# Weight parts of K/V tile 0 re-sorted over GpSimd and VectorE, batch 3's x measured in batch 2, and tile 1's products ahead of both h rows

## The reference, cut to what matters

```
mod = (silu(c) @ wmod).reshape(B, 6, 1, D);  sa, ca, ga, sb, cb, gb = mod[:, 0..5]
h  = layernorm(x) * (1 + ca) + sa
Xn = layernorm(h) * gamma + beta;  Q, K, V = split(Xn @ W_in + b_in)
K, V = rotary(K), rotary(V)
A  = 0.5 * sum_over_rows(K/|K| * V/|V|) + 0.5          # one vector of 512 per batch
x  = x + ga * ((A * Q) @ W_out + b_out + h)
h  = layernorm(x) * (1 + cb) + sb
x  = x + gb * (relu(h @ W_up.T) @ W_down.T + sum(softmax(top2(h @ W_gate.T))) * (h @ W_expert))
```

## Time and profile before

| | |
|---|---|
| median of 3 runs | 363.78 us (363.32 to 365.0) |
| profiled execution, its own time | 365.14 us |
| its span, first to last instruction | 363.4 us |
| TensorE busy (matmul) | 353.1 us, 97% |
| TensorE weight loads | 288.5 us, 79% |
| VectorE / ScalarE / GpSimd | 247.9 / 159.1 / 126.6 us |
| granted TensorE clock | 1.000 over the whole span |

### The profile page before, as it was taken

The page is one execution under the profiler, slowest core; times in us unless marked ns, Lnnn a source line. Parts: engine busy times, 40 slices in busy tenths (PEclk is TensorE's granted clock), DMA queues, the critical chain, the costliest instruction groups (busy, mean ns, idle before and its releaser), DMA issues.

```text
span 363.4 us, 4952 instructions
## 1 busy us (share of the span) xinstructions
PE 353.1 (97%) x1794; PEld 288.5 (79%) x1794; DVE 247.9 (68%) x508; ACT 159.1 (44%) x301; POOL 126.6 (35%) x131
## 2 busy tenths in 40 slices
PE   8799999999999999999999999999999999999996
PEld 5257587788777788888888898988988898889885
DVE  2689999979977778786977469338623852382474
ACT  1296838647169501476018753444234423441110
POOL 0395879777726166243531324800100010000000
PEclk9999999999999999999999999999999999999999
DMA  6998482370120000000000003101100110011003
GB/s 182 388 406 317 194 318 89 137 213 0 25 63 2 0 2 29 1 1 2 0 31 0 0 2 115 32 0 58 60 0 2 58 59 2 0 60 58 2 1 115
DMA packets 10985, 27.45 MB, mean 76 GB/s; under 512 B 1216, under 2 KB 1600, under 8 KB 9808
## 3 DMA queue, kind: packets, MB, share of 16 engines
q1 hardware_dynamic: 10960, 27.13, 21.1%
HBM read 22.90 MB, written 4.23 MB: 75 GB/s over the span
## 4 chain that ended last, share of the span: by engine, by line
PE 60%; DVE 12%; ACT 8%; issue 7%; DMA 5%; POOL 5%; SPq 2%; POOLq 0%; DVEq 0%; ACTq 0%
PE ps L1225 19%; PE ps L1227 19%; PE ps L1226 19%; PE ps L1284 2%; DMA gate_bc<-mod_rows 2%; DMA xs<-in_X 2%; POOL w_lo L414 2%; DVE hb L815 1%; DVE hst L825 1%; ACT z L626 1%; POOL hrs L411 1%; ACT ps L638 1%; DMA mod_rows<-xs 1%; ACT ps L585 1%; ACT z L617 1%
## 5 line engine op out<-in xcount | busy, mean ns | idle before, releaser
L1225 PE MATMUL ps<-wv_hi,t_hi 128*128 128x260 f32 (+1 forms) x192 | 61.7, 322 | 0.9 <-POOL wv_lo L414 0.5
L1227 PE MATMUL ps<-wv_hi,t_lo 128*128 128x260 f32 (+1 forms) x192 | 61.4, 320 | 0.0
L1226 PE MATMUL ps<-wv_lo,t_hi 128*128 128x260 f32 (+1 forms) x192 | 61.4, 320 | 0.0
L1225 PE MATMUL ps<-w_hi,g_hi 128*128 128x512 f32 (+1 forms) x132 | 51.2, 388 | 0.0
L1225 PE MATMUL ps<-t_hi,w_hi 128*128 128x512 f32 x128 | 50.6, 396 | 0.1
L1227 PE MATMUL ps<-w_hi,g_lo 128*128 128x512 f32 (+1 forms) x132 | 50.6, 383 | 0.0
L1226 PE MATMUL ps<-w_lo,g_hi 128*128 128x512 f32 (+1 forms) x132 | 50.6, 383 | 0.0
L1227 PE MATMUL ps<-t_hi,w_lo 128*128 128x512 f32 x128 | 50.0, 390 | 0.0
L1226 PE MATMUL ps<-t_lo,w_hi 128*128 128x512 f32 x128 | 49.9, 390 | 0.0
L1225 PEld LDWEIGHTS ps<-wv_hi,t_hi 128*128 128x128 f32 x192 | 36.1, 188 | 5.1 <-POOL wv_lo L414 1.4
L411 POOL TENSOR_TENSOR hrs<-hve,expo 128x4 f32<-128x4 f32 (+2 forms) x12 | 11.1, 923 | 81.9 <-DVE hve L832 62.8
(11 more groups left out here) (153 smaller groups left out, 703.8 us busy)
## 6 DMA issues: line engine op xcount, KB each, us to landing
stage<-in_w SPq DMA_DIRECT2D x5, 1024.0 KB, 4.8
out<-xs SPq DMA_DIRECT2D x15, 256.0 KB, 2.0
xs<-in_X SPq DMA_DIRECT2D x3, 1024.0 KB, 9.5
xs<-in_wmod SPq DMA_DIRECT2D x8, 256.0 KB, 5.9
stage<-in_w SPq DMA_DIRECT2D x8, 256.0 KB, 8.1
xs<-in_wmod SPq DMA_DIRECT2D x2, 1024.0 KB, 7.7
gate_bc<-mod_rows SPq DMA_DIRECT2D x8, 256.0 KB, 3.9
gate_bc<-in_wmod SPq DMA_DIRECT2D x1, 1024.0 KB, 13.3
```

The lines of the kernel that those rows point to most:

```text
L1225: mm(dst, l_hi, r_hi, start=start, stop=False)
L1226: mm(dst, l_hi, r_lo, start=False, stop=False)
L1227: return mm(dst, l_lo, r_hi, start=False, stop=stop)
```

## The change

Three edits come together.

1. In K/V tile 0 of batch 0 ScalarE rounds V's chunk 0 ahead of the first normalisation, K's chunk 1 ahead of the first evacuation and V's chunk 1 right behind it. GpSimd takes the lower part of K's chunk 1 ahead of `rstd_x0(2)`. The lower part of V's chunk 3 goes from GpSimd to VectorE, behind row tile 3's `h_row0`.
2. x of batch 3 is measured by VectorE in batch 2, as x of batch 2 is in batch 1: four statistics between the lower query parts, aggregation, shift after tile 0's products; ScalarE normalises it after tile 0's sums of squares of batch 2. ScalarE's two passes and the small steps are gone, and `rstd_x(3)` stands on GpSimd at the end of batch 1, behind `base`.
3. In batches 1 and 2 `h_row(b + 1, 0)` stands behind `kv_products(b, 1)`, with the other three, and no longer between `kv_sum(b, 0)` and `kv_rows(b, 1)`.

```
 GpSimd, attention(b)
                     weight(b, 1)
-                    if b + 2 < B:
-                        rstd_x(b + 2)
                     rstd_h(b + 1, 0, NT)
...
                         base(b + 1, t)
+                    if b == 1:
+                        rstd_x(3)
 GpSimd, start
             shift_h0(1)
+            low_kv(0, 1)
             rstd_x0(2)
-            low_kv(0, 1)
             low_kv(1, 1)
             low_kv(1, 2)
             low_kv(0, 3)
-            low_kv(1, 3)
             shift_h0(2)
 ScalarE, attention(b)
-                if b == 1:
-                    normalise_x(2)
-                    x_sums()
-                    x_squares()
+                if b < B - 1:
+                    normalise_x(b + 1)
                 norm_sums(b, 1)
...
-                if b + 2 < B:
-                    normalise_x(b + 2)
 ScalarE, start
             split_hi_kv(0, 0)
+            split_hi_kv(1, 0)
             normalise(0, 0, 1)
-            split_hi_kv(1, 0)
+            split_hi_kv(0, 1)
             t0_evac(0)
-            split_hi_kv(0, 1)
+            split_hi_kv(1, 1)
             normalise(0, 1, 1)
-            split_hi_kv(1, 1)
 VectorE, attention(b)
                     q_split(b - 1, c)
-                    if b == 1:
-                        x_row_stats(2, c)
-                if b == 1:
-                    x_aggr(2)
+                    if b < B - 1:
+                        x_row_stats(b + 1, c)
+                if b < B - 1:
+                    x_aggr(b + 1)
                 kv_rows(b, 0)
                 kv_products(b, 0)
-                if b == 1:
-                    x_shift(2)
+                if b < B - 1:
+                    x_shift(b + 1)
...
                 finish_rows(b - 1)
-                if b == 1:
-                    x_mean()
                 kv_sum(b, 0)
-                if b < B - 1:
-                    h_row(b + 1, 0)
-                else:
+                if b == B - 1:
...
                 kv_rows(b, 1)
-                if b == 1:
-                    x_var()
                 kv_products(b, 1)
                 if b < B - 1:
+                    h_row(b + 1, 0)
                     h_row(b + 1, 1)
...
                 kv_products(b, 2)
-                if b + 2 < B:
-                    x_shift(b + 2)
                 kv_sum(b, 2)
 VectorE, start
             h_row0(3)
+            split_lo_kv(1, 3)
             t0_split(1)
```

More of the change, by code:

```diff
@@ L102, in build @@
         nmu = xmn
-        xss = sb("xss", [P, NT])
         xst = sb("xst", [P, NT, 6])
@@ L116, in build @@
         sqj = sb("sqj", [P, D], mybir.dt.bfloat16)
-        xjunk = sb("xjunk", [P, D], mybir.dt.bfloat16)
         a_col = sb("a_col", [P, NC])
@@ L181, in build @@
         base_s = sem("base_s")
-        xsum_s = sem("xsum_s")
-        xmn_s = sem("xmn_s")
         kv_ps, kb_s, kv_sb = sem("kv_ps"), sem("kb_s"), sem("kv_sb")
@@ L589, in t0_evac @@
                                      ACT.Copy).then_inc(t_his, 1)
[L591 to L605, removed]
             def normalise_x1(t):
@@ L788, in x_aggr @@
                 v.tensor_scalar(xve[:], xmv[:, :, 1], EPS, None, ALU.add).then_inc(xve_s, 1)
[L790 to L797, removed]
             def x_shift(g):
@@ L801, in x_shift @@
                 wait(dve, xn_s, (g - 1) * NT)
-                if g < B - 1:
-                    v.scalar_tensor_tensor(xnm[:], xmv[:, :, 0], -1.0, xrs[:], ALU.mult, ALU.mult).then_inc(xnm_s, 1)
-                else:
-                    dve.wait_ge(xmn_s, 1)
-                    v.tensor_tensor(xnm[:], xmn[:], xrs[:], ALU.mult).then_inc(xnm_s, 1)
+                v.scalar_tensor_tensor(xnm[:], xmv[:, :, 0], -1.0, xrs[:], ALU.mult, ALU.mult).then_inc(xnm_s, 1)
             def h_row(g, t):
@@ L1078, in split_lo_kv @@
                 dve.wait_ge(wlo_v if i else wlo_k, k)
+                dve.wait_ge(wlo_v if i else wlo_k, k)
                 v.tensor_tensor(w_lo_of(W_ORDER[i], k), w_raw[i][:, k * D:(k + 1) * D],
```

## The result

| | before | changed kernel |
|---|---|---|
| median, 20 runs each, beside each other | 364.46 us (362.38 to 365.32) | 365.07 us (363.73 to 365.5) |
| ratio, 95% interval | | 1.0021 (1.0011 to 1.0031) |
| profiled execution: own time, span | 365.14, 363.4 | 363.73, 361.9 |
| VectorE / ScalarE / GpSimd busy | 247.9 / 159.1 / 126.6 | 249.3 / 153.5 / 124.7 |

The account below looks back on a forecast made before the run. TensorE (97% busy) bounds the kernel; only holes between its weight loads can be won. Arrival +0.2, batch 1 -1.0, batch 2 +0.35 sum to -0.4 us: profiled 365.14 to 364.7, median 363.78 to 363.4; range 361.3 to 365.3.

Parts of the forecast that it names:

- batch 1: -1.0 us forecast: Batch 1's total: -0.46 - 0.12 - 0.43 = -1.0 us, with ends -0.4 and -2.7.
- the moved work costs: Rival: VectorE loses the turn at 35.4, moved h row loses one at 90.5, batch 2 pays +0.6; +0.8, 364.6; chance 0.26.
- the turn at 35.4: Tile 0's product step against GpSimd's first scaling: VectorE first gives -0.2 us, GpSimd first loses 0.6.
- the wait for the gates: VectorE's wait for gates from DRAM; ending over 1 us away from 79.5 would show the forecast wrong.
- K/V tile 0: Batch 0's first tile: V 3 loads at 27.9 instead of 28.50; TensorE leaves about 0.5 us earlier, not 2.1.
- What arrives at batch 1: Delay or lead carried from tile 0 to batch 1's transposes: +0.2 us, with ends -0.5 and +1.1.
- -1.24: Batch 1, tile 3: the 1.28 us hole closes; about 0.8 of the 1.24 us is given back.
- -0.46: Batch 1, transposes at 105.93 for batch 2: 0.46 us earlier if VectorE's product step is first; hole grows to 1.6.
- +0.14: Batch 1, product step at 90.56: if GpSimd is first, the variance comes at 99.36, 0.14 us later; not taken.
- -0.12: Batch 1, 110.30: the x shift in front of tile 2's sum is gone, -0.12 us.
- -0.43: Batch 1's last lower query part comes 0.7 us earlier, closing the 0.47 us hole: -0.43 us.
- +0.35: Batch 2: h row behind tile 1's products costs at the second transposes, hole 0.21 becomes 0.5; ends 0 and +0.7.

Follow-up runs that it names:

- e11: e6 with rstd_x0(2) back in front of the lower part of K's chunk 1; 363.77 us, ratio 1.0000.
- e14: e13 with h_row(b+1, 0) back in front of tile 1; 362.81 us, ratio 0.9966.
- e5: Kernel before plus one tiny GpSimd product ahead of out_weight(1)'s subtraction, so VectorE is first at 57.7 us; 363.53 us, ratio 0.9986.
- e16: e14 without the K/V tile 0 part of the change; 363.44 us, ratio 0.9984.
- e4: Kernel before with only batch 3's x measured by VectorE in batch 2; 364.52 us, ratio 1.0001.
- e13: e6 with the 1 MB load of batch 3's x moved behind batch 3's modulation rows; 363.59 us, ratio 0.9986.
- e1: The changed kernel again, unaltered; 364.90 us, ratio 1.0018 to before.
- e6: Changed kernel plus the tiny GpSimd product of e5, so VectorE is first at 57.7 us; 363.97 us, ratio 1.0001.
- e8: Changed kernel plus the two tiny VectorE instructions of e7; 365.24 us, ratio 1.0026.
- e7: Kernel before plus two tiny VectorE instructions ahead of the weighted sum, so GpSimd is first at 57.7 us; 364.73 us, ratio 1.0019.
- e12: Kernel before with out_weight(1) behind weight(0, 3) on GpSimd, without a tiny instruction; 364.72 us, ratio 1.0019.

## Why the prediction was wrong

It forecast -0.4 us; it is +0.6 by the medians and +0.8 by the means. The step that failed is batch 1: -1.0 us forecast, +0.26 measured. Two terms were put at nothing, the toss at 57.7 us (about +0.3) and the end of the program (+0.29). The rival "the moved work costs" had the right sign. Of its three places the moved row in batches 1 and 2 was right; the turn at 35.4 was not lost: the changed kernel's product step there takes 0.29 us as before. It was won by a hair, with VectorE's step 0.01 us ahead of GpSimd's scaling, but in all ten traces with edit 1. One of the prediction's own signs of being wrong came true as well: the wait for the gates was to end within 1 us of 79.5, and the residual started at 77.28.

**K/V tile 0: right.** V's part 2 starts on GpSimd at 23.33, K's part 2 ends on VectorE at 25.18, V 3 loads at 27.37 with all times 0.45 us earlier than before from the start on (transposes at 17.51 against 17.96); forecast 23.8, 25.6, 27.9. Missed was that the first product comes 0.57 us later relative to those transposes, since a small VectorE step now lies behind GpSimd's split of K's part 1. The changed kernel, VectorE and GpSimd in tile 0 (timeline):

```profile
19.86 1.17 DVE L1011 TENSOR_SCALAR xve<-xmv 128x2 f32<-128x2 f32 x1
...
24.23 0.95 DVE L1035 TENSOR_TENSOR w_lo<-stage,w_hi 128x512 fp32r<-128x512 f32 x1
...
26.61 0.70 DVE L1035 TENSOR_TENSOR wv_lo<-stage,wv_hi 128x512 fp32r<-128x512 f32 x1
...
19.73 1.26 POOL L410 TENSOR_TENSOR w_lo<-stage,w_hi 128x512 fp32r<-128x512 f32 x1
...
23.33 1.31 POOL L410 TENSOR_TENSOR wv_lo<-stage,wv_hi 128x512 fp32r<-128x512 f32 x1 [0.26 <-ACT wv_hi L572]
...
26.59 0.55 POOL L407 TENSOR_TENSOR hrs<-hve,expo 128x1 f32<-128x1 f32 x1
```

**What arrives at batch 1: a term left out.** VectorE won the turn at 35.4, so the -0.2 of that order was there (transposes(1,0) 38.14 us after the first ones, 38.40 before). But I followed the edit only up to the transposes at 56.36 and took the end of batch 0 as it stood in one execution. There, at 57.7, lies a toss worth 1.2 us, which VectorE wins in about 44% of before's executions and in 16 to 22% of the changed kernel's. This term, about +0.3 on the mean, had no place in the sum, and the row that would have warned stood in the trace: two engines 0.05 us apart, one of them with a length of two turns. My ends for this part (+1.1) held its size, but for another meeting.

**Batch 1: the step that failed, wrong in sign, for two reasons.** The -1.24 at tile 3 and the -0.46 that was to be left of it rested on a hole that this execution had because its residual had waited 1.46 us for the gates. Of the 17 other traces 15 have no such wait, and without it there is no hole at tile 3 to close, with the h row in either place. VectorE then idles 2.67 us for TensorE with edits 2 and 3, where the forecast had 1 us, and +0.26 to +0.28 is lost. But the wait alone would not have saved it. e11 has a wait of 0.94 us and the moved row (timeline, VectorE, then weight loads):

```profile
79.15 1.29 DVE L881 TENSOR_TENSOR hb<-ps,hb 128x512 f32<-128x512 f32 x2 [0.94 <-DMA gate_bc<-mod_rows]
...
87.95 0.70 DVE L819 TENSOR_TENSOR ps<-ps,bkv_bc 128x512 f32<-128x512 f32 x1 [1.64 <-PE ps L1187]
...
90.77 0.83 DVE L836 TENSOR_TENSOR ps<-prod 128x128 f32<-128x128 f32 x1
91.98 3.02 DVE L780 TENSOR_TENSOR hb<-hb,sa_bc 128x512 f32<-128x512 f32 x2
```

```profile
105.68 0.86 PEld L1244 LDWEIGHTS ps<-idn,z 128*128 128x128 f32 x8 [1.59 <-ACT z L608]
```

Here the rows start 8.80 us after the residual, a microsecond sooner than elsewhere, and yet the transposes for batch 2 come 26.53 us after it, 0.11 later than with the h row in its old place. The product step is not first (0.83 us instead of 0.29) and the two rows lose another turn (3.02 instead of 1.27). The hole before the transposes is 1.59 us, close to the 1.6 that the forecast had for an execution with the wait. But the order is that of the branch which the prediction priced at +0.14 and did not take: I gave VectorE a tie on the strength of 0.04 us of replay.

**-0.12 and -0.43: not there.** From (2,0) to (2,2) it is 4.37 to 4.38 us with and without the x shift. The hole of 0.47 did close, but it was given back by batch 2's second transposes. With edit 2, VectorE's residual of batch 2 no longer waits for TensorE, its second gate step loses a turn (1.46 us against 0.79) and the first h row behind tile 1 waits for half a turn: 1.32 us in e14 at 138.42, where e5 has (timelines of e5, VectorE and weight loads):

```profile
127.45 0.69 DVE L919 TENSOR_TENSOR hb<-ps,hb 128x512 f32<-128x512 f32 x1 [0.57 <-PE ps L1230]
...
139.92 0.68 DVE L818 TENSOR_TENSOR hb<-hb,sa_bc 128x512 f32<-128x512 f32 x1
```

```profile
120.98 0.19 PEld L1228 LDWEIGHTS ps<-w_hi,g_hi 128*128 128x128 f32 x1 [0.45 <-DVE g_lo L910]
...
155.64 0.89 PEld L1287 LDWEIGHTS ps<-idn,z 128*128 128x128 f32 x8 [0.17 <-issue]
```

From (2,2) to (3,2) the kernel without edits 1 to 3 (e5) takes 47.05 us and e16, which has edit 2, 47.14: nothing is left of the 0.43. e4's ratio of 1.0001 says the same, within its interval of 0.5 us to either side.

**Batch 2: right in size.** +0.35 forecast for the moved row, +0.28 measured (47.22 - 46.94, e13 and e14); the hole forecast at 0.5 is 0.70, the rest being what edit 2 gives back.

**Sum by its terms**, forecast against the traces: tile 0 and arrival +0.2 against -0.26 (the order of the -0.2), batch 1 -1.0 against +0.26 up to the first transposes for batch 2, batch 2 +0.35 against about +0.1 from (2,2) to (3,2), where the -0.43 is given back and the moved row costs (47.21 to 47.24 in the changed kernel, e1, e6, e8 and e13; 47.05 to 47.26 in before, e5, e7 and e12), the toss nothing against about +0.3, the end of the program nothing against +0.29. The measured terms add up to about +0.7, against +0.78 for the means.

## What to carry to other kernels

Before costing an edit, look in the trace for meetings in which two engines ask for the port almost together (here 0.05 us apart), and ask of every one behind the edit what the other order would cost: such a meeting makes two kernels out of one, and an edit that does not touch it can still change how often it is won. One tiny instruction on the engine that should lose fixes the order, here for 1.2 us. A hole behind a wait whose length is set by a DMA is no basis for a replay from one execution: take a second trace of the kernel before and see whether the hole is there. Work moved out of a gap in which its engine only waits for TensorE was free there and costs where it goes, here 0.26 to 0.28 us of its 0.60 per batch. And compare the stretch behind the last work too, since an edit can lengthen it.

## What the hardware showed beyond that

- A power on GpSimd does not hold VectorE, which the forecast had assumed from the earlier trace rows: VectorE's split at 26.61 took 0.70 us over the power at 26.59, its length when alone (0.68). The other way round a power does wait: GpSimd's power for 128x4 at 144.87 in e5 took 1.71 us beside VectorE's sum at 144.70, where the one of the earlier trace rows took 1.01. The Trainium skill, "SBUF — State Buffer", section "Who interferes with whom", calls the shared port pair an exclusive lock; by that, as an estimate from the power's end at 27.14, this split would have been 0.5 us longer, and the trace does not agree for this instruction.
- A scalar VectorE step on 128x2 elements took 1.17 us at 19.86 beside GpSimd's split at 19.73, so even the smallest of these pays a whole turn (the same step took 0.17 us at 20.31 in the trace of before).
- The slowest of four equal transfers of 256 KB took 4.5 to 7.5 us with a load of 1 MB issued 0.53 us behind it, and 3.9 to 4.2 us without.
- One GpSimd operation less in the whole program (130 instead of 131) goes with an end of the program that is 0.29 us longer.
